# Selective-scan macaron block on one core: every sequence scanned by half of its columns, the residual product kept in PSUM, layer statistics issued in pieces

## The reference

```python
x = x + 0.5 * ffn(layernorm(x), w_gate, w_up, w_down)      # x: (16, 1024, 256) fp32
x = x + attn(layernorm(x), ...)
x = x + 0.5 * ffn(layernorm(x), w_gate, w_up, w_down)

def ffn(x):                     # hidden 768, weights int / 127
    return (silu(x @ wg.T) * (x @ wu.T)) @ wd.T

def attn(x):                    # a selective scan, 256 channels e, 16 states n
    z, params = x @ W_z.T, x @ W_params.T
    dt = softplus(params[..., :64] @ W_dt.T + b_dt)
    C = params[..., 80:]
    u = silu(depthwise causal conv of x, 4 taps)
    A = -exp(A_log);  a = exp(dt * A);  B = (a - 1) / A
    h[0] = B[0] * u[0];  h[t+1] = a[t] * h[t] + B[t] * u[t]
    y = sum over n of C[t, n] * h[t, :, n] + u * D
    return (y * silu(z)) @ W_out.T
```

## Time and profile before

| | |
|---|---|
| median of 3 runs | 2453.26 us (2450.96 to 2454.65) |
| profiled execution | 2457.36 us, its span 2455.6 us |
| mean granted TensorE clock | 0.956 |
| busy share of the span: DVE, PE, POOL, ACT | 93%, 92%, 84%, 83% |

### The profile page before, as it was taken

The page is one execution under the profiler, slowest core; times in us unless marked ns, Lnnn a source line. Parts: engine busy times, 40 slices in busy tenths (PEclk is TensorE's granted clock), DMA queues, the critical chain, the costliest instruction groups (busy, mean ns, idle before and its releaser), DMA issues. The chain is left out here.

```text
span 2455.6 us, 28769 instructions
## 1 busy us (share of the span) xinstructions
PE 2258.3 (92%) x9220; PEld 1359.8 (55%) x9220; DVE 2282.8 (93%) x2454; ACT 2030.5 (83%) x2926; POOL 2073.5 (84%) x1286
## 2 busy tenths in 40 slices
PE   6977999999999999999999999999999999999578
PEld 3443656556565555656556565655656555565346
DVE  2599999999999999999999999999999999999993
ACT  4888888988888797988989888898888889898662
POOL 1588988989898898889989898898988889899873
PEclk9997999999999899999999899999999999999789
DMA  2122433434343343434434243343434334333221
GB/s 68 49 78 59 135 130 129 138 126 139 106 154 130 120 139 112 145 116 142 140 122 146 100 149 130 129 138 129 138 106 151 131 129 138 122 129 114 84 65 39
DMA packets 112027, 291.21 MB, mean 119 GB/s; under 512 B 11201, under 2 KB 45314, under 8 KB 111874
## 3 DMA queue, kind: packets, MB, share of 16 engines
q1 hardware_dynamic: 111874, 289.35, 35.7%
HBM read 271.49 MB, written 17.83 MB: 118 GB/s over the span
## 5 line engine op out<-in xcount | busy, mean ns | idle before, releaser
L996 POOL TENSOR_TENSOR acc<-acc,ring 128x1024 f32<-128x1024 f32 x512 | 1209.5, 2362 | 146.7 <-DVE ring L1178 134.2
L1142 DVE TENSOR_TENSOR_SCAN g_bank<-du_bank,ring 128x1024 f32<-128x1024 f32 (+1 forms) x512 | 1100.6, 2155 | 7.3 <-ACT du_bank L903 0.5
L674 PE MATMUL work<-wd_t,hid 128*128 128x256 f32 x3072 | 697.7, 386 | 37.1 <-DVE hid L1099 35.5
L1178 DVE SCALAR_TENSOR_TENSOR ring<-g_bank,inv_a,ring 128x1024 f32<-128x1024 f32 (+1 forms) x576 | 664.6, 1159 | 11.4
L674 PEld LDWEIGHTS work<-wd_t,hid 128*128 128x128 f32 x3072 | 590.0, 193 | 153.4 <-DVE hid L1099 43.6
L921 ACT ACTIVATE ring<-dt,a_coef 128x1024 f32<-128x1024 f32 (+1 forms) x576 | 577.4, 1047 | 7.0 <-DVE g_bank L1142 4.1
L742 ACT ACT_TABLE_LOAD x289 | 370.8, 1283 | 5.1
L662 PE MATMUL work<-xt_hi,wu_t 128*128 128x512 f16 x768 | 304.9, 397 | 26.9 <-ACT xt_lo L793 14.4
L662 PE MATMUL work<-xt_hi,wg_t 128*128 128x512 f16 x768 | 299.7, 390 | 29.4 <-ACT sil L806 14.5
L662 PE MATMUL work<-xt_lo,wu_t 128*128 128x512 f16 x768 | 304.3, 396 | 0.0
L662 PE MATMUL work<-xt_lo,wg_t 128*128 128x512 f16 x768 | 298.8, 389 | 0.0
(11 more groups left out here) (96 smaller groups left out, 2797.9 us busy)
## 6 DMA issues: line engine op xcount, KB each, us to landing
ring<-c_rows SPq DMA_DIRECT2D x448, 512.0 KB, 3.6
ring<-c_rows SPq DMA_DIRECT2D x64, 256.0 KB, 3.1
x_in<-L_attn_x SPq DMA_DIRECT2D x30, 512.0 KB, 5.4
out<-x_fin SPq DMA_DIRECT2D x30, 512.0 KB, 5.2
c_rows<-params SPq DMA_DIRECT2D x32, 32.0 KB, 3.0
x_fin<-L_attn_x SPq DMA_DIRECT2D x2, 512.0 KB, 4.4
out<-x_in SPq DMA_DIRECT2D x2, 512.0 KB, 2.9
ring<-L_ffn_w_gate SPq DMA_DIRECT2D x1, 768.0 KB, 5.8
```

Of the source, the lines that this page charges most:

```text
L674: last = pe.matmul(dst[:, j * E:(j + 1) * E], hid[:, K.unit[f, bt, c, m] % HIDS, t:t + P], wd_t[:, m, :], start=(m == 0), stop=(m == HM - 1))
L996: nc.gpsimd.tensor_tensor(v, v, shaped(bt, cg[:, K.number[ev[1:]] % TERMS, :]), ALU.add).then_inc(S["summed"], 1)
L1142: scan = nc.vector.tensor_tensor_scan(g, du_h, d_h, first[0], ALU.add, ALU.mult)
L1178: nc.vector.scalar_tensor_tensor(v, g, inv_a[:, h, s:s + 1], c_row, ALU.mult, ALU.mult).then_inc(S["weighted"], 1)
```

## The change

`paired` is true for all rows, so rows 1 to 14 are now scanned as rows 0 and 15 were. `ai` keeps only the product, which it writes back into its own bank; a new event `aj` makes `acc` from u and the bank, and frees it. The four `bn_stats` of a norm are events `sj` of their own. All three tables are new numbers. Waits are moved accordingly.

```diff
 def paired(b):

-    return b in (0, B - 1)
+    return True
...
+            elif kind == "ln":
+                made = [place["sj", ev[1], ev[2], ev[3], j] for j in range(TJ)] + [place[ev]]
+                assert made == sorted(made)
...
         return ({"ga": "si", "dn": "rs", "op": "rc", "z": "zs", "pm": "pe", "cv": "us", "dt": "da",
-                 "rm": "ai"}[job[0]],) + job[1:]
+                 "rm": "aj"}[job[0]],) + job[1:]
...
                     wait(act, "du", ("d", bt - 2, EH - 1))
-                    wait(act, "acc_begun", ("ai", bt - 2, EH - 1, NC - 1))
+                    for k in range(EH * NC):
+                        wait(act, "free", ("rm", bt - 2, k // NC, k % NC))
...
-                    wait(act, "ready", ("rm", bt - 1, EH - 1, c))
+                    for h in range(EH):
+                        wait(act, "ready", ("dt", bt - 1, h, c))
+                        wait(act, "ready", ("rm", bt - 1, h, c))
...
                     if s == 0:
                         for k in range(EH):
-                            wait(pool, "acc_begun", ("ai", bt, k, p) if paired(bt) else ("ai", bt, p, k))
+                            wait(pool, "free", ("rm", bt, k, p) if paired(bt) else ("rm", bt, p, k))
...
-                    if kind == "ln":
-                        _, f, bt, c = ev
-                        slot = K.at["meanvar", ev][1] % 2
+                    if kind == "sj":
+                        _, f, bt, c, j = ev
+                        unit = ("ln", f, bt, c)
+                        slot = K.at["meanvar", unit][1] % 2
...
+                        before = K.prev["meanvar", unit]
+                        if len(before) >= 2:
+                            wait(dve, "meanvar", before[-2])
+                        nc.vector.bn_stats(stats[:, slot, j, :], src[:, c * TJ + j, :]).then_inc(S["stats"], 1)
+                    elif kind == "ln":
+                        slot = K.at["meanvar", ev][1] % 2
+                        wait(dve, "stats", ("sj",) + ev[1:] + (TJ - 1,))
...
-                        nc.vector.tensor_tensor(t, bank(job)[:], u[bt % 2][:, h, 1 + c * CH:1 + (c + 1) * CH],
-                                                ALU.mult).then_inc(freed(job), 1)
-                        wait(dve, "free", job)
-                        nc.vector.scalar_tensor_tensor(t, u[bt % 2][:, h, 2 + c * CH:2 + (c + 1) * CH], d_skip[:, h:h + 1], t,
-                                                       ALU.mult, ALU.subtract).then_inc(S["acc_begun"], 1)
+
+                        nc.vector.tensor_tensor(bank(job)[:], bank(job)[:], u[bt % 2][:, h, 1 + c * CH:1 + (c + 1) * CH],
+                                                ALU.mult).then_inc(S["times_u"], 1)
+                    elif kind == "aj":
+                        _, bt, h, c = ev
+                        job = ("rm",) + ev[1:]
+                        wait(dve, "times_u", ("ai",) + ev[1:])
+                        nc.vector.scalar_tensor_tensor(acc[bt % 2][:, h, c * CH:(c + 1) * CH],
+                                                       u[bt % 2][:, h, 2 + c * CH:2 + (c + 1) * CH], d_skip[:, h:h + 1],
+                                                       bank(job)[:], ALU.mult, ALU.subtract).then_inc(freed(job), 1)
```

A pair of lines of the tables:

```diff
-    "ai": [-4.711, -5.166, -4.862, -3.977],
+    "ai": [-2.825, -5.783, -4.96, -2.936],
+    "aj": [-1.355, -5.305, -4.254, -2.819],
```

More of the change, by code:

```diff
@@ L77 @@
 ROW = {
[59 rows of a table removed]
-    "gate": [18.529, 32.88],
-    "scan": [0.419, 2.279, 3.308, 4.253, 5.467, 5.732, 5.845, 6.028, 6.566, 8.77, 9.768, 10.708, 11.528, 13.09,
-        13.729, 14.444, 16.014, 16.934, 18.934, 19.764, 20.59, 21.249, 22.033, 23.423, 23.709, 24.128, 26.114,
-        26.965, 28.267, 28.803, 29.667, 30.466],
-    "cm": [1.741, 2.589, 3.841, 5.159, 5.503, 5.826, 5.929, 6.453, 7.619, 9.297, 9.95, 11.411, 11.894, 13.582,
-        14.339, 14.979, 16.464, 18.234, 18.981, 19.901, 20.734, 21.395, 22.8, 23.693, 24.097, 25.061, 26.47, 27.503,
-        28.635, 29.584, 30.268, 32.083],
@@ L150 @@
-    "op": [35.343, 35.563, 38.067, 38.279],
-    "rc": [34.543, 34.806, 36.425, 37.971],
-    "ra": [34.196, 35.385, 37.281, 40.898],
[64 rows of a table added]
+    "gate": [17.95, 33.497],
+    "scan": [0.557, 1.785, 2.373, 3.515, 5.148, 5.701, 5.852, 6.508, 7.558, 8.652, 9.817, 10.454, 10.896, 13.613,
+        13.882, 14.658, 16.722, 17.009, 18.131, 18.601, 20.335, 21.688, 21.859, 23.651, 24.264, 24.345, 24.983,
+        26.252, 28.425, 29.614, 29.879, 31.163],
+    "cm": [1.557, 1.882, 3.498, 3.894, 5.689, 5.752, 6.155, 7.201, 8.049, 9.059, 10.205, 10.843, 12.615, 13.617,
+        14.629, 14.923, 16.865, 17.148, 18.217, 19.101, 21.652, 21.698, 22.828, 24.18, 24.271, 24.77, 25.878, 27.462,
+        28.531, 29.819, 30.568, 32.003],
@@ new lines @@
+    "bc": [-1.875, -0.839, -0.772, -0.283, -0.07, 0.931, 3.132, 4.96, 5.354, 5.827, 9.244, 9.957, 10.638, 12.036,
+        12.04, 13.065, 14.075, 15.778, 16.512, 16.597, 16.831, 18.838, 20.264, 21.883, 22.718, 23.666, 23.761,
+        25.148, 25.227, 25.29, 25.991, 27.764],
+    "ex": [-1.172, 0.045, 0.282, 0.36, 3.823, 4.692, 5.108, 5.773, 5.899, 5.93, 5.993, 6.985, 8.301, 9.068, 11.848,
+        12.018, 12.421, 12.529, 13.053, 13.133, 13.381, 19.4, 19.934, 19.941, 21.403, 21.815, 22.126, 22.877, 22.963,
+        25.175, 28.498, 28.682],
@@ L153 @@
+    "op": [35.185, 35.75, 36.699, 37.829],
+    "rc": [33.442, 34.114, 37.505, 38.608],
+    "ra": [34.342, 35.36, 37.327, 41.453],
 }
 HEAD = {
-    "ln1": [-97.354, -42.071],
-    "lr1": [-68.526, -65.946],
-    "ls1": [-53.313, -40.38],
-    "lx1": [-71.151, -44.852],
-    "T1": [-66.235, -33.668],
-    "Te1": [-67.922, -35.768],
-    "Ts1": [-64.153, -32.686],
-    "Tl1": [-51.682, -34.546],
-    "ln2": [-25.298, -5.26],
-    "lr2": [-15.536, -0.533],
-    "ls2": [-14.486, -0.053],
-    "lx2": [-21.006, -0.277],
@@ L240, in row_events @@
         for c in range(NC):
+            for j in range(TJ):
+                yield f"sj{f}", ("sj", f, b, c, j)
             for kind in ("ln", "lr", "ls", "lx", "T", "Te") + (("Ts", "Tl") if f != 2 else ()):
@@ L257, in row_events @@
         for c in range(NC):
-            for kind in ("cv", "us", "z", "zs", "dt", "da", "dl", "dp", "rm", "ai"):
+            for kind in ("cv", "us", "z", "zs", "dt", "da", "dl", "dp", "rm", "ai", "aj"):
                 yield kind, (kind, b, h, c)
@@ L367, in releaser @@
         return ({"ga": "si", "dn": "rs", "op": "rc", "z": "zs", "pm": "pe", "cv": "us", "dt": "da",
-                 "rm": "ai"}[job[0]],) + job[1:]
+                 "rm": "aj"}[job[0]],) + job[1:]
     def increments(self, ev):
         kind = ev[0]
+        if kind == "sj":
+            return [("stats", 1)]
         if kind == "ln":
-            return [("stats", 1), ("meanvar", 1)]
+            return [("meanvar", 1)]
         if kind == "Te":
@@ L384, in increments @@
             return [(f"c_out{ev[2]}", 16)]
-        one = {"db": "du_in", "gate": "gated", "u0": "u_first", "dt0": "dt_first", "ai": "acc_begun",
+        one = {"db": "du_in", "gate": "gated", "u0": "u_first", "dt0": "dt_first", "ai": "times_u",
                "d": "du", "da": "sp_exp", "dl": "sp_ln", "dp": "sp_sum", "si": "silu",
@@ L1071, in program @@
                         elif f == 2:
-                            wait(dve, "mid_added", ("rp", bt, c, 1))
+                            wait(dve, "mid_added", ("rp", bt, c, j // 2))
                         else:
-                            wait(dve, "fin_added", ("ra", bt, 2 * c + 1))
+                            wait(dve, "fin_added", ("ra", bt, 2 * c + j // 2))
+                        before = K.prev["meanvar", unit]
[5 more added lines that the diff above has]
+                        wait(dve, "stats", ("sj",) + ev[1:] + (TJ - 1,))
                         before = K.prev["meanvar", ev]
@@ L1078, in program @@
                             wait(dve, "normed", ("lx",) + before[-2][1:])
-                        for j in range(TJ):
-                            last = nc.vector.bn_stats(stats[:, slot, j, :], src[:, c * TJ + j, :])
-                        last.then_inc(S["stats"], 1)
-                        wait(dve, "stats", ev)
                         for j in range(TJ):
@@ L1112, in program @@
                         hold(dve, w_landed, LANDED)
-                        t = acc[bt % 2][:, h, c * CH:(c + 1) * CH]
                         wait(dve, "ready", job)
```

34 lines of the change are left out of this document (removed), and 203 rows, old and new, of tables (HEAD, ROW, TAIL).

## The result

| | before | after |
|-|-|-|
| median of 5 runs each, us | 2453.33 | 2469.01 |
| lowest to highest | 2450.96 to 2454.65 | 2463.03 to 2474.15 |
| ratio, 95% interval | 1 | 1.0065, 1.0044 to 1.0086 |
| a middle row (mean of rows 1 to 13, first scan to first scan), us | 145.4 | 146.7 |
| DVE busy / idle in it | 141.8 / 3.6 | 142.1 / 4.6 |

The change makes the kernel 0.65% slower, where I forecast 1% faster; 2469 us lies outside the range of 2403 to 2464. The profiled execution of after took 2474.15 us, the slowest of the five.

The account below looks back on a forecast made before the run. DVE's own sequence was taken to bound the kernel from first to last scan. +42 - 71 - 9 + 14 = -24 us on the profiled 2457.4 gave 2433, or 2429 us as median; range 2403 to 2464.

Parts of the forecast that it names:

- The bound: From the first scan to 2405 us, DVE's own sequence sets the time; DVE 97.5% busy in rows 1 to 14.
- Pairing, +42 us: Rows 1 to 14: paired scan and `cm` units cost DVE 3.0 us more a row, +42 us.
- the rival of a fixed cost paid in full: Every small DVE instruction pays its fixed cost without overlap, 4.0 us a paired unit: about 2565 us; chance 0.03.
- The product, -71 us: All rows: four `ai` and `aj` pairs take DVE 4.8 us instead of 9.5 a row, counted as -71 us.
- the rival of a stretched `aj`: `aj` is stretched by GpSimd's work as before, giving -8 us in place of -71: 2492 us; chance 0.04.
- Statistics, -9 us: Norms on DVE: five of six broken up by other work, saving 0.6 us a row, -9 us.
- ScalarE, +14 us: Rows 1 to 14: more ACT work, costed only as added DVE stalls, +1.0 us a row, +14 us.
- My cover, the slack of ACT: ACT's work lies beside DVE's and costs nothing as work; its slack falls from 20 to about 9 us a row.
- The upper bound of +3.5 us: Highest value given for added DVE stalls a row in rows 1 to 14, where the whole gain is eaten.
- ScalarE makes it slower: ACT's work plus 14 us of unavoidable waits makes a row 148.2 us, +38 us, 2490 us; chance 0.10.
- Other queues, 0: PE, POOL, SP's broadcasts and the longer-held bank of `rm` add nothing; PE runs several jobs ahead of DVE.
- Signs I named: Middle rows 143 to 144 us, units 3.61 and 3.66, `aj` and `ai` 0.68, DVE above 97%, ACT 93%.

Follow-up runs that it names:

- E1: The kernel before with only the product kept in its bank, tables and units as before: 2427.99 us, ratio 0.989 to before.
- E5: The changed kernel with one exponential of 1024 columns per paired unit instead of two of 512, group 0's coefficients for both: 2423.29 us, ratio 0.9864 to before.
- E7: E1 with each exponential of 1024 columns in rows 1 to 14 made as two of 512: 2474.99 us, ratio 1.0091 to before.
- E9: The changed kernel with ACT's copy `sp_v` left out, so softplus's correction has another value: 2441.41 us, ratio 0.9956 to before.
- E10: E1 with ACT's two copies of the parameters made one, 0.8 us less of ACT a row: 2426.18 us, ratio 0.9892 to before.
- E2: The changed code with the tables of before, statistics pieces together and `aj` right behind `ai`: 2506.32 us, ratio 1.0192 to before.
- E11: E2 with one exponential per unit instead of two, group 0's coefficients for both groups: 2490.02 us, ratio 1.0149 to before.
- E4: The changed kernel with `aj` right behind `ai` in all rows, so the bank is freed at once: 2481.69 us, ratio 1.0104 to before.
- E8: E1 with the first of a middle row's four products moved one place later: 2429.14 us, ratio 0.9889 to before.
- E14: E1 with the last of a middle row's four products moved one place later: 2429.41 us, ratio 0.9893 to before.
- E13: E1 with two of the convolution's four taps left out, 6.9 us of PE work a row: 2435.79 us, ratio 0.9917 to before.

## Why the prediction was wrong, point by point

| us a row | forecast | measured |
|-|-|-|
| paired units | +3.0 | +3.3 |
| product in its bank | -4.7 | -4.4 |
| statistics in pieces | -0.6 | -0.8 |
| `ls`, same instruction | 0 | +0.6 |
| DVE's waits | +1.0 | +2.6 |
| sum | -1.3 | +1.3 |

The measured terms are distances from start to start, waits taken out, in rows 1 to 13 of the two traces; the row itself grew by 1.3 us, and 13 such rows are the 16 us of the medians.

- **The bound.** "DVE's own sequence sets the time" was nearly true of before (waits of 1.9 us in 145.4) and too strong as a rule for the changed kernel. I read 97.5% busy as full. E1 shows what was under it: 4.0 us less of work gained only 2.1, and then a second bound stood at 143.3 us.
- **Pairing, +42 us.** Right as DVE's work in the new order, within 0.3 us a row: 3.61 and 3.67 us a unit in middle rows. The overlap of independent neighbours that I took from the last row holds everywhere, so the rival of a fixed cost paid in full (Trainium skill, VectorE: DVE Perf Modes, TRN2 errata), 4.0 us a unit, is out.
- **The product, -71 us.** Right as DVE's work, `aj` 730 ns everywhere; the rival of a stretched `aj` is out. Wrong as time: E1 gained 27. (My own terms, 62 products at 1.19 us, make -74; the -71 was a slip.)
- **Statistics, -9 us.** Right as DVE's work; no run has them alone. Not forecast: `ls`, whose neighbours changed.
- **ScalarE, +14 us: the step that failed.** I wrote "its slack falls from 20 to about 9 us ... some of it will come back as stalls", and put +1.0 us a row on it. ACT went from 125.4 to 133.4 us as computed (134.2), and DVE's waits rose by 2.6 us. DVE's own work, from start to start, fell by 1.3 us a row, less than the 2.3 forecast, and would still have made the kernel faster; the waits turned that round. E5 and E7 give the price of the exponentials by themselves: 5.5 us of busy ACT a row are 3.2 to 3.5 us of row, 46 and 47 us of time, three times the whole term that I had for ACT. My cover, the slack of ACT, was an average: ACT has 13 us idle a row in after and is yet in the way, because PE's jobs need its short products at given moments: PE waits 5.5 us a row for ACT in after, 3.4 before and 3.0 in E5. The upper bound of +3.5 us held the waits; I chose near the low end because DVE was the engine others waited for.
- **The rivals.** What happened is "ScalarE makes it slower", at less than half of its size: +16 us, where I gave +38 and a chance of 0.10. I had made it a threshold: nothing to pay until ACT's work and unavoidable waits fill the row. In after that isn't so, ACT has 13 us idle and is paid for. Nor is there one price: for each us of ACT's busy time it is 0.6 us of row in E5 and in E7, 1.0 in E9, 0.2 in E10 and 0.1 from E2 to E11.
- **Other queues, 0.** The held bank cost about nothing in the row (E4). Ahead of the first scan and behind the last row: 0 forecast, 102.1 to 102.3 and 50.7 to 50.5 us measured.
- **Signs I named.** Middle rows of 143 to 144 us: 146.7. Units and `aj`, `ai`: as said. DVE above 97%: 97.0. ACT at 93% with half the waits for PE: 91%, its waits for PE 16.7 us a row before and 12.1 now. DVE's waits above 3 us a row, my sign of a wrong last step: 4.6 us.

**What stays open.** What holds E1 at 143.3 us: it isn't the place of one product (E8, E14), and 0.8 us less of ACT's gives 0.15 us of row (E10). A loop over ACT, PE and DVE and PE's clock are both left (E13 changed work and clock together), and I have no run that parts them. E1's trace has the clock right ahead of the wait: PE is at half clock from 1367.4 to 1374.2 us, which costs it at most 3.4 us, an estimate; its matmuls for the last product start at 1375.86, and DVE waits 3.21 us for them. Nor do I know how much of ACT's price in after is the two further table loads and how much the exponentials; a kernel with the new order and the old number of loads wasn't run.

## What to carry to other kernels

Where three engines stand above 85% and feed each other, the busiest one's work is not the time: price what the change adds to the second and third as well, and don't count their idle time as cover. Here each us on ACT cost 0.6 us in the two cleanest experiments and 0.1 to 1.0 in the others, so it has to be measured in the kernel at hand. A gain on the busiest engine holds only down to the next bound, so run the gain alone first; here it was the better kernel by 1.7%. A table of orders fitted for one code is part of it: the same tables, with the statistics in pieces, gave 37 us to the paired code and made the unpaired code the slowest of all.
